# ScalarE writes the SiLU itself and Tanh of the half input gives its derivative, in the test-time MLP of an eight-layer kernel

## What is computed

```
def _mlp(params, h):
    W1, b1, W2, b2 = params
    return jax.nn.silu(h @ W1 + b1) @ W2 + b2
...
def step(params, kvt):
    k_t, v_t = kvt
    g = jax.grad(loss_fn)(params, k_t, v_t)
    new_params = tuple((p - LR * gp for p, gp in zip(params, g)))
    return (new_params, None)
params, _ = jax.lax.scan(step, (W1, b1, W2, b2), (k, v))
q = x @ W_Q
return _mlp(params, q)
```

## Time and profile before

| | us |
|---|---|
| three runs | 2525.14, 2526.87, 2530.11 (median 2526.87) |
| the profiled execution, its own time | 2527.97 |
| its span in the profile | 2526.2 |
| the 32 chunks, first Sigmoid to last weight update | 509.75 to 869.17 |
| TensorE busy, over the span | 2047.0 (81%) |
| VectorE busy | 1839.3 (73%) |
| ScalarE busy | 1284.7 (51%) |
| GpSimd busy | 569.2 (23%) |

### The profile page before, as it was taken

How to read it: one execution, slowest core, us unless ns; L and a number is a source line. 1 busy time by engine, 2 the same in 40 slices (tenths; PEclk the granted TensorE clock), 3 DMA queues, 4 the chain that set the end, 5 groups by cost and what they waited for, 6 DMA issues and landing times.

```text
span 2526.2 us, 63931 instructions
## 1 busy us (share of the span) xinstructions
PE 2047.0 (81%) x20012; PEld 1151.2 (46%) x20012; DVE 1839.3 (73%) x3701; ACT 1284.7 (51%) x2711; POOL 569.2 (23%) x1161
## 2 busy tenths in 40 slices
PE   4459885788888688649999996659999999999745
PEld 3336552567777553324444444413333333333534
DVE  4866767755556458748888886669999999999471
ACT  4321115633333230236777774538888888888511
POOL 4322233134444310201111111001111111111303
PEclk9755557999999979869999998869999999999876
DMA  2342210000000000031111110131111111111001
GB/s 57 83 123 70 70 45 18 8 0 0 0 0 0 1 9 0 12 112 33 32 32 32 37 26 4 46 86 39 38 38 38 38 38 38 39 39 33 22 0 33
DMA packets 140882, 86.62 MB, mean 34 GB/s; under 512 B 67338, under 2 KB 120211, under 8 KB 140756
## 3 DMA queue, kind: packets, MB, share of 16 engines
q1 hardware_dynamic: 140756, 84.95, 13.6%
HBM read 57.01 MB, written 27.26 MB: 33 GB/s over the span
## 4 chain that ended last, share of the span: by engine, by line
PE 50%; DVE 16%; ACT 5%; issue 5%; DMA 1%; SPq 1%; POOL 1%; DVEq 0%; POOLq 0%; ACTq 0%; PEldq 0%
PE psum L2282 13%; PE psum L2260 11%; PE psum L2271 8%; DVE ba_blockmax L2525 5%; DVE X L1424 2%; PE psum L2291 2%; ACT tt_sg L1786 1%; DVE tt_aT L1841 1%; PE psum L1745 1%; PE psum L1754 1%; PE psum L1352 1%; PE psum L1735 1%; SPq L2187 1%; DVE row_stats L148 1%; PE psum L1764 1%
## 5 line engine op out<-in xcount | busy, mean ns | idle before, releaser
L2525 DVE TENSOR_REDUCE ba_blockmax<-psum 128x16 f32<-128x1024 f32 x512 | 602.4, 1218 | 35.5 <-PE psum L2260 32.8
L2364 ACT ACTIVATE ba_pt<-psum 128x512 f32<-128x512 f32 x1024 | 550.6, 598 | 71.1 <-PE psum L2271 52.9
L2260 PE MATMUL psum<-ba_ks,ba_qs 64*128 64x512 bf16 x1024 | 341.9, 414 | 40.2 <-DMA ba_ks<-ba_kstk 20.1
L2527 DVE TENSOR_REDUCE sa_negmax<-psum 128x1 f32<-128x1024 f32 x256 | 304.3, 1221 | 85.2 <-PE psum L2260 77.4
L2364 ACT ACTIVATE sa_pt<-psum 128x512 f32<-128x512 f32 x512 | 269.8, 599 | 115.8 <-PE psum L2271 113.0
L2282 PE MATMUL psum<-ba_pt,ba_vh 128*32 128x256 f32 x4096 | 314.3, 390 | 0.1
L2271 PE MATMUL psum<-ba_qs,ba_ks 64*128 64x512 bf16 x1024 | 313.6, 381 | 0.8 <-ACT ba_pt L2364 0.8
L2260 PE MATMUL psum<-sa_ks,sa_qs 96*128 96x512 bf16 x512 | 206.7, 409 | 27.7 <-DMA sa_ks<-sa_kstk 24.2
L2260 PEld LDWEIGHTS psum<-ba_ks,ba_qs 64*128 64x128 bf16 x1024 | 113.1, 149 | 231.8 <-issue 229.1
L2271 PE MATMUL psum<-sa_qs,sa_ks 128*128 128x512 bf16 x512 | 193.8, 382 | 1.5 <-ACT sa_pt L2364 1.5
L2282 PEld LDWEIGHTS psum<-ba_pt,ba_vh 128*32 128x32 f32 x4096 | 92.3, 108 | 154.5 <-issue 146.6
(11 more groups left out here) (454 smaller groups left out, 3883.7 us busy)
## 6 DMA issues: line engine op xcount, KB each, us to landing
ba_qs<-ba_qstk SPq DMA_DIRECT2D x128, 48.0 KB
ba_ks<-ba_kstk SPq DMA_DIRECT2D x128, 48.0 KB
dn_pst<-dn_arena SPq DMA_DIRECT2D x32, 128.0 KB, 2.5
dn_tst<-dn_arena SPq DMA_DIRECT2D x8, 512.0 KB, 5.8
dn_arena<-dn_tst SPq DMA_DIRECT2D x8, 512.0 KB, 4.2
dn_arena<-dn_pst SPq DMA_DIRECT2D x8, 512.0 KB, 6.4
ba_qs<-ba_qstk SPq DMA_DIRECT2D x128, 32.0 KB
ba_ks<-ba_kstk SPq DMA_DIRECT2D x128, 32.0 KB
```

The lines of the kernel that those rows point to most:

```text
L2260: last = nc.tensor.matmul(bank(2 * slot + h), qs[b][0:KP, :].rearrange("p (a r) -> p r a", r=NTB)[:, r, :], ks[b][0:KP, h * HALF:(h + 1) * ...
L2364: nc.scalar.activation(pt[x_][:, :, h * P:(h + 1) * P].rearrange("p j (a m) -> p j a m", m=2), bank(4 + slot).rearrange("p (a j m) -> p j ...
L2525: ins = nc.vector.tensor_reduce(blockmax[g][:, r, :], src.rearrange("p (n s) -> p n s", s=BLOCK), AXX, ALU.max, negate=True)
L2527: ins = nc.vector.tensor_reduce(negmax[g][:, r:r + 1], src, AXX, ALU.max, negate=True)
```

## The change

ScalarE applies two functions to h in place of one: Silu, straight into `tt_aT`, and Tanh of (h + b1)/2 into `tt_sg`, which now holds 2·sigmoid - 1. VectorE's gate product L1841 is left out. With t = tanh the derivative times two is (1 + t) - (t - 1)·silu, so tsp keeps its form, sp becomes (sg + 1) - tsp, and the factor in dh is halved. The halved bias for Tanh is a new column, `tt_b1h`, written by VectorE after each chunk's weight update; Tanh of a chunk's first sweep waits for it.

```
-                    nc.scalar.activation(sg[:, :], bank(HB)[:, 0:P], ACT.Sigmoid, bias=b1).then_inc(self.sig, 1)
+                    nc.scalar.activation(aT[:, :], bank(HB)[:, 0:P], ACT.Silu, bias=b1).then_inc(self.a, 1)
+                    if s == 0:
+                        a.wait_ge(self.half_b1, c + 1)
+                    nc.scalar.activation(sg[:, :], bank(HB)[:, 0:P], ACT.Tanh, bias=b1h[:, :], scale=0.5).then_inc(self.sig, 1)
...
                     v.wait_ge(self.sig, n + 1)
-                    nc.vector.scalar_tensor_tensor(aT[:, :], bank(HB)[:, 0:P], b1, sg[:, :], ALU.add, ALU.mult).then_inc(self.a, 1)
                     v.wait_ge(self.a, n + 1)
                     nc.vector.scalar_tensor_tensor(tsp[:, :], sg[:, :], -1.0, aT[:, :], ALU.add, ALU.mult).then_inc(self.t_own, 1)
                     v.wait_ge(self.t_own, n + 1)
-                    nc.vector.tensor_tensor(sp[:, :], sg[:, :], tsp[:, :], ALU.subtract).then_inc(self.sp, 1)
+                    nc.vector.scalar_tensor_tensor(sp[:, :], sg[:, :], 1.0, tsp[:, :], ALU.add, ALU.subtract).then_inc(self.sp, 1)
...
-                    nc.vector.scalar_tensor_tensor(r[:, 3 * P:4 * P], bank(DB)[:, 0:P], -ETA, r[:, 0:P], ALU.mult, ALU.mult).then_inc(self.dh, 1)
+                    nc.vector.scalar_tensor_tensor(r[:, 3 * P:4 * P], bank(DB)[:, 0:P], -ETA / 2, r[:, 0:P], ALU.mult, ALU.mult).then_inc(self.dh, 1)
...
                 nc.vector.tensor_tensor(ws[:, W1N:WN], ws[:, W1N:WN], bank(WB)[:, 0:WN - W1N], ALU.add).then_inc(self.weights2, 1)
+                half_bias(c + 1)
+
+            def half_bias(c):
+                v.wait_ge(self.weights1, c + 1)
+                nc.vector.tensor_scalar(b1h[:, :], b1, 0.5, None, ALU.mult).then_inc(self.half_b1, 1)
```

More of the change, by code:

```diff
@@ L1478, in test_time_mlp @@
     diff, dsum, vsum, sqr = (k.sb(f"tt_{n}", [P, R], ctx=ctx) for n in ("diff", "dsum", "vsum", "sqr"))
+    b1h = k.sb("tt_b1h", [P, 1], ctx=ctx)
     verdict = k.sb("tt_verdict", [P, 6], ctx=ctx)
@@ L1693, in __init__ @@
              self.weights1, self.weights2, self.p_own) = (k.sem(f"ttf_{n}") for n in names)
-            self.table = k.sem("ttf_table")
+            self.table, self.half_b1 = k.sem("ttf_table"), k.sem("ttf_half_b1")
             self.sp, self.judged = k.free_sem("ttf_sp"), k.free_sem("ttf_judged")
@@ L1773, in scalar @@
         def scalar(self, a):
-            nc.scalar.activation(sgq[0][0:1, 0:1], k.mhalf[0:1, 0:1], ACT.Sigmoid).then_inc(self.table, 1)
+            nc.scalar.activation(sgq[0][0:1, 0:1], k.mhalf[0:1, 0:1], ACT.Silu).then_inc(self.table, 1)
             a.wait_ge(self.table, 1)
@@ L1869, in first @@
                 nc.vector.tensor_copy(ws[:, W1N:WN], w0[:, W1N:WN]).then_inc(self.weights2, 1)
+                half_bias(0)
             self.chunks(v, first, body)
```

## The result

| | before | changed |
|---|---|---|
| four runs each, us | 2525.14 to 2530.11, median 2527.54 | 2512.22 to 2515.34, median 2513.43 |
| span of the profiled execution | 2526.2 | 2510.5 |
| a chunk, behind the first | 11.20 | 10.82 |
| its three sweeps | 3.29, 3.45, 4.46 | 3.20, 3.45, 4.16 |

The changed kernel takes 0.9945 of the time of the one before (95% interval 0.9927 to 0.9962), 14 us less. The forecast was 2515, within 2509 to 2523.

What follows compares the result with a forecast made beforehand. Sp's transpose through dh bounds the third sweep, GpSimd's L1823 holding tsp the second. 32 x (0.29 + 0.08) = 11.8 us, table loads 0, from the median 2526.87 to 2515 us; range 2509 to 2523.

Steps and rivals of the forecast that it cites:

- The halved bias: First sweep: L1865 starts between 0.10 and 0.19 and takes 0.17, Tanh waits for it and starts at 0.30.
- Silu and Tanh at Sigmoid's price, overlapped: ScalarE, each sweep: both activations take 0.37, Tanh starting at 0.27 before Silu ends; tsp starts 0.11 us earlier.
- The rival of a Tanh that doesn't overlap: ScalarE: Tanh starts at 0.40, which costs 0.14 us a chunk, 4.5 us in all, 2522.4; chance 0.12.
- that of a dearer Silu: ScalarE: Silu takes double, 0.74, a chunk is 0.37 us longer and the kernel 11.8 slower, 2539; chance 0.04.
- Third sweep 0.29: Third sweep of each chunk: sp's transpose moves from 1.69 to 1.34, dh from 2.47 to 2.18, 0.29 us gained.
- a queue part and a tsp part: Third sweep's 0.29: 0.11 from tsp's earlier start, 0.18 from TensorE's queue no longer holding back sp's transpose.
- First and second sweep 0.08: First sweep's sp comes 0.08 us earlier, GpSimd's chain too; the second sweep gains nothing beyond that.
- the tie to GpSimd: Second sweep: tsp on VectorE cannot finish until GpSimd's L1823 ends, and itself ends 0.15 us after it.
- The rival with a fixed price of 0.21: Second sweep: working beside GpSimd costs a fixed 0.21; a chunk gains 0.55, 17.6 us in all, 2509; chance 0.08.
- The rival in which the bias is caught by GpSimd: First sweep: GpSimd delays the halved bias, Tanh starts at 0.41; the change gives 8.3 us, 2518.5; chance 0.15.
- Table loads at zero: Query part: two new table loads of 1.28 us on ScalarE cost 0, hidden by waits; without that cover 2.6.
- The sum: Whole stage: 32 chunks times (0.29 + 0.08) make 11.8 us gained.

## Why the prediction was right

- **Silu and Tanh at Sigmoid's price, overlapped.** Taken: 0.37 each, Tanh at 0.27. Measured: 0.37, 0.36 and 0.26 to 0.27. The rival of a Tanh that doesn't overlap and that of a dearer Silu fall by these rows alone.
- **Third sweep 0.29.** Measured 0.30, at the places named: transpose at 1.33 (said 1.34), dh at 2.17 (2.18). The split into a queue part and a tsp part was shown from both sides, by taking the queue out of the kernel before (0.17) and by putting it back into the changed one (0.17).
- **First and second sweep 0.08.** Measured 0.09, and all of it in the first. That the tie to GpSimd decides was shown by releasing it in both kernels. The rival with a fixed price of 0.21 said a tsp of 0.50; it took 0.65, ending again 0.15 behind GpSimd. The Trainium skill's rule of an exclusive claim ("SBUF — State Buffer", section "Who interferes with whom") is borne out by that row.
- **The halved bias.** Said to start between 0.10 and 0.19 and to take 0.17; it started at 0.11 and took 0.15, while GpSimd's L1818 was still running (637.67 to 638.49). Tanh then started at 0.29, said 0.30. The rival in which the bias is caught by GpSimd fell: its one column was not held up.
- **Table loads at zero.** This is the step that failed. The prediction let the first load start with the weight product, so that load and copy would be over while TensorE still waited for VectorE's `tt_b2row`. The load started 0.88 later, when that product was through, and TensorE's next product came 0.6 us later than before. The second load's cover held.
- **The sum.** 32 times 0.37 said 11.8; the stage gave 12.6 in the profile, of which 0.9 came in the first chunk, where it was 12.18 before and 11.25 now. I had counted it at the common 0.37. Its length varies between 11.3 and 12.2 in the other kernels, and it starts at TensorE's low clock (0.50 from 509.75 to 512 us before). The remaining distance between 11.8 and the measured 14 is less than the interval of the ratio (9.6 to 18.5 us).
- **Luck in the total.** The sum was made for the stage, and the stage bears it out. That the whole time came within 2 us of it as well is in part luck: in the profiles the query part cost 2.9 us that the prediction had at nothing, and 5.7 us less were spent ahead of the stage and behind the query part, in code that is the same.

## What to carry to other kernels

Ask of a loop of short dependent steps, iteration by iteration, which wait ends last: three sweeps with the same code had three different limits here, and one edit gave them 0.09, nothing and 0.30 us. Where a step stretches, look for the instruction of another engine that ends a fixed time ahead of it in every iteration: a gain in front of such a tie is only a longer wait until the tie is moved. A function-table load at a join of branches can stand behind the very wait that should hide it, and a one-element activation ahead of that wait moves it.

## What I had not expected of the hardware

An instruction with two waits started 0.07 us later when one of them was the last to come than when the other was. tsp started 0.03 behind Tanh in the changed kernel and 0.10 behind Silu (639.59 to 639.69) with the order turned round, in every sweep of both; Silu's `ttf_a` stands first in the listing of its waits and is the last one written in the code. dh in the kernel before, whose `ttf_rows_a` stands so too, started 0.10 behind the copy in the second and third sweeps and 0.04 behind da, as the profile models its end, where da was the last, in the first. That it is the place of the wait is what these two have in common; no run changed the place alone. And the query part, whose products and gates are the same in the kernel before and in most of those above, took from 28.5 to 34.1 us, which is more than any edit there was worth. The granted clock in its first 14 us was 0.60 or lower in every profile in which it took over 31 us, and above 0.75 in every one in which it took under 30. The rise to full clock came 4.9 to 6.8 us behind the weight product in the seven short ones, 11.1 to 11.7 in three (31.6 to 31.9 us long) and 17.1 in the other three (33.5 to 34.1), and in none between these.
